# Routing and attention fetches rearranged: most tiles of x read during attention, half of the statistics on ScalarE, groups of 4, 4, 4, 4, 8, 8, one weight load a step, half rows read ahead

## The reference

```
x = x + proj(attention(layernorm(x)))          # 16 heads of 16, rotary, causal mask
z = layernorm(x)
e = argmax(z @ centroids.T)                     # 8 experts, one for each token
y = z + relu(LN_e(z) @ w1[e].T + b1[e]) @ w2[e].T + b2[e]     # 256 -> 1024 -> 256
x = x + alpha * y + (1 - alpha) * z,   alpha = sigmoid(z @ centroids[e])
```

## Time and profile before

| | us |
|---|---|
| median of 3 runs (878.6 to 885.98) | 881.75 |
| the profiled execution | 886.25 |
| its span | 884.5 |
| PE busy | 812.1 |
| DVE busy | 599.5 |
| ACT busy | 508.4 |
| POOL busy | 340.6 |

### The profile page before, as it was taken

The page is one execution under the profiler, slowest core; times in us unless marked ns, Lnnn a source line. Parts: engine busy times, 40 slices in busy tenths (PEclk is TensorE's granted clock), DMA queues, the critical chain, the costliest instruction groups (busy, mean ns, idle before and its releaser), DMA issues. The chain is left out here.

```text
span 884.5 us, 24359 instructions
## 1 busy us (share of the span) xinstructions
PE 812.1 (92%) x8788; PEld 497.3 (56%) x8789; DVE 599.5 (68%) x1161; ACT 508.4 (57%) x1175; POOL 340.6 (39%) x476
## 2 busy tenths in 40 slices
PE   7999859889979999999999988777999999999984
PEld 4555423333334444443344335456999999999853
DVE  5888999779969999999999605754733333333342
ACT  4767427668858888888888892023333333333331
POOL 9999653233333433334343332524111111133211
PEclk9999979999989999999999999988899999999998
DMA  7578532543453343433335115865555555555550
GB/s 281 179 231 255 170 119 69 175 169 53 111 106 91 95 100 97 90 87 86 86 81 159 51 42 180 277 189 196 173 186 182 180 180 183 187 187 189 179 173 4
DMA packets 63355, 128.90 MB, mean 146 GB/s; under 512 B 16982, under 2 KB 44247, under 8 KB 56983
## 3 DMA queue, kind: packets, MB, share of 16 engines
q1 hardware_dynamic: 59094, 112.53, 42.9%
q0 software_dynamic: 4160, 15.03, 4.6%
HBM read 99.89 MB, written 22.98 MB: 139 GB/s over the span
## 5 line engine op out<-in xcount | busy, mean ns | idle before, releaser
L917 ACT ACTIVATE arena<-ps_pair 128x512 f32<-128x512 f32 (+2 forms) x640 | 317.9, 556 | 76.6 <-PE ps_pair L1240 73.7
L997 DVE TENSOR_REDUCE B_block_max<-ps_item 128x8 f32<-128x1024 f32 x288 | 335.4, 1217 | 37.4 <-PE ps_item L1144 37.1
L1240 PE MATMUL ps_pair<-q_stack,k_stack 99*32 99x512 bf16 (+7 forms) x3072 | 198.5, 334 | 9.4 <-DMA q_stack<-B_nm 6.7
L831 POOL TENSOR_SCALAR_AFFINE_SELECT arena<-arena 128x256 f32<-128x256 f32 x256 | 102.4, 409 | 160.2 <-ACT arena L917 158.5
L1257 PE MATMUL ps_pair<-arena,B_v_quad 128*32 128x512 f32 (+3 forms) x1536 | 157.0, 493 | 0.9 <-ACT B_oacc L936 0.7
L1240 PEld LDWEIGHTS ps_pair<-q_stack,k_stack 99*32 99x32 bf16 (+1 forms) x3072 | 69.1, 96 | 130.0 <-ACT arena L917 62.1
L2037 PEld LDWEIGHTS C_bank<-arena 128*128 128x128 f32 x1024 | 122.5, 196 | 5.2 <-ACT arena L1558 3.7
L2037 PE MATMUL C_bank<-arena 128*128 128x128 f32 x1024 | 123.0, 280 | 2.0 <-ACT arena L1558 2.0
L1144 PE MATMUL ps_item<-k_stack,q_stack 64*128 64x128 bf16 (+2 forms) x1280 | 108.2, 267 | 15.9 <-DVE B_block_max L997 8.9
L2061 PE MATMUL C_ps_p<-arena 128*128 x512 | 117.4, 381 | 3.2 <-issue 3.1
L1588 ACT ACTIVATE arena<-C_bank,ffn_columns 128x128 f32<-128x128 f32 x128 | 36.6, 368 | 116.8 <-PE C_bank L2037 108.0
(11 more groups left out here) (204 smaller groups left out, 777.0 us busy)
## 6 DMA issues: line engine op xcount, KB each, us to landing
arena<-in_w_exp SPq DMA_DIRECT2D x41, 1024.0 KB
qk_parts<-arena SPq DMA_DIRECT2D x32, 384.0 KB, 3.4
q_stack<-qk_parts SPq DMA_DIRECT2D x96, 128.0 KB, 3.3
k_stack<-qk_parts SPq DMA_DIRECT2D x64, 128.0 KB, 3.4
arena<-in_w_exp POOLq DMA_DIRECT2D x6, 1024.0 KB, 7.1
rows<-payload SPq DMA_DIRECT2D x32, 130.5 KB
arena<-in_x SPq DMA_DIRECT2D x8, 512.0 KB, 4.7
arena<-in_x_feat SPq DMA_DIRECT2D x8, 512.0 KB, 5.7
```

What stands on the lines that cost most here:

```text
L831: pool.affine_select(out=block_p, in_=block_p, compare_op=ALU.is_ge, fill=0.0, base=0, pattern=[[0, 2], [1, P]], channel_multiplier=-1).th ...
L917: act.activation(pr[s % PR][:, h:h + 2 * n - 1:2, 0:W], ps_s[(EXPS * Q.const + exps_to[s] + u) % R][:, 0:n * W].rearrange("p (h n) -> p h ...
L997: dve.tensor_reduce(bmx[:, g:QH:GH, first:first + 3 * gap + 1:gap], src[:, :, :].rearrange("p c (b n) -> p c b n", n=P), AX.X, ALU.max).th ...
L1240: mm = pe.matmul(bank[at:at + 32, :], ks[rows, r, half, bass.ds(g * SEQ + kb * P + at, 32)], qs[rows, r, half, bass.ds(g * SEQ + c * QW + ...
```

## The change

- `GROUPS` is (4, 4, 4, 4, 8, 8), not (4, 4, 4, 4, 6, 6, 4); four groups are scattered within the loop over pairs, the other two from slots 0 and 1. The token numbers (`COL_ID`) are copied group by group, before each group's scatters.
- Of the 32 tiles of x, 24 are read in step 14 of attention, in three transfers of 1 MB: two into a ring slot of the q and k stacks that is free by then, one into the last sequence's values (`load_early`). `add` reads them there. The other 8 tiles are read in the routing stage, now behind `place_out`, `store_inverse` and `spread_inverse` of step 15. b2 is read once four pairs are added.
- `stats` of the even pairs 0 to 14 go to ACT: an ACTIVATE Copy for the mean and an ACTIVATE Square for the variance of each tile, with accumulation, and one to scale the means.
- DVE inverts step 15's sums at pair 4 (was 2) and normalizes the last outputs at pair 10 (was 7).
- In attention, `place_out(n-2)` comes behind the maxima of step n in SP's queue. The pad regions are written three each in steps 5, 7 and 9, between `spread_inverse` and `load`. w2 is read in steps 1, 2, 3, 4, 5 and 14, at sub-block 4.
- Rows of half slots have a buffer each and are read in steps 24 to 30, before `load_rows` would read them.
- The first normalization (slot 0) stands ahead of the last pair of ACT's statistics; the table's scratch rows are in another tile.

```diff
-GROUPS = (4, 4, 4, 4, 6, 6, 4)
+GROUPS = (4, 4, 4, 4, 8, 8)
...
+        def load_early(sp):
+
+            sp.wait_ge(s_vq, NQ)
+            for i in range(3):
+                sp.dma_start(x_early[i][:, :, :], x[i * KB * P:(i + 1) * KB * P, :].rearrange("(t p) n -> p t n", p=P)).then_inc(s_early[i], 16)
...
+        def load_half_rows(sp, k):
+            at = sp.value_load(slot_tab[0:1, 1, bass.ds(FULL + k, 1)], min_val=0, max_val=DUMMY_ROW + HT)
+            sp.dma_start(half_rows[:, k, 0:P],
+                         pay_d[bass.ds(at, HT), 0:DIM].rearrange("t (a n) -> a t n", a=DC)).then_inc(s_rh[k], 16)
+            sp.dma_start(half_rows[:, k, P:P + PAYW - DIM],
+                         pay_d[bass.ds(at, HT), DIM:PAYW].unsqueeze(0).to_broadcast([DC, HT, PAYW - DIM])).then_inc(s_rh[k], 16)
...
-        early_at = (1, 1, 2, 2, 14, 14)
+        early_at = (1, 2, 3, 4, 5, 14)
+        W2_AT = 4
...
-                    if n.const >= 2:
-                        place_out(sp, n.const - 2, out_ring(n.const - 2))
                     if n.within(NQ):
 
                         wait(sp, s_n3, n, 1, 1)
                         for half in range(2):
                             sp.dma_start(qs[SROWS[half]:SROWS[half] + MROWS, n.ring(R), half, :],
                                          nm[half * MAXR // 2:(half + 1) * MAXR // 2, :]).then_inc(s_row, 16)
+                    if n.const >= 2:
+                        place_out(sp, n.const - 2, out_ring(n.const - 2))
                     if n.const == 2:
                         load_bias_rows(sp)
-                    if n.const == 4:
-                        sp.wait_ge(s_pad0, 2)
-                        for e in range(NE + 1):
-                            sp.dma_start(pay_d[e * REGION:e * REGION + P, :], padrow).then_inc(s_pad, 16)
                     if n.const >= 3:
                         spread_inverse(sp, n.const - 3)
+                    if n.const in (5, 7, 9):
+                        if n.const == 5:
+                            sp.wait_ge(s_pad0, 2)
+                        for e in range(3 * (n.const - 5) // 2, 3 * (n.const - 5) // 2 + 3):
+                            sp.dma_start(pay_d[e * REGION:e * REGION + P, :], padrow).then_inc(s_pad, 16)
                     Q = n + 2
                     if Q.within(NQ):
                         load(Q)
+                    if Q.const == NQ:
+                        wait(sp, s_s, Q, QH * SUB, -QH * SUB * (R - 1))
+                        load_early(sp)
...
-                        if k == NM_AT + 1:
+                        if k == W2_AT:
...
+        BY_ACT = [u for u in range(NP - 1) if u % 2 == 0]
...
-                    t = h * G // 2
+                place_out(sp, NQ - 1, o_last)
+                store_inverse(sp, NQ - 1)
+                spread_inverse(sp, NQ - 1)
+                for h in range(len(s_x)):
+                    t = X_LATE + h * G // 2
                     sp.dma_start(xr[:, t:t + G // 2, 0:DIM],
                                  x[t * P:(t + G // 2) * P, :].rearrange("(t p) n -> p t n", p=P)).then_inc(s_x[h], 16)
-                    if h == 0:
-                        place_out(sp, NQ - 1, o_last)
-                    if h == 4:
-                        store_inverse(sp, NQ - 1)
-                    if h == 5:
-                        spread_inverse(sp, NQ - 1)
                 sp.dma_start(col[:, :, :], cols).then_inc(s_fl, 16)
+                sp.wait_ge(s_x2, KB // 2)
                 sp.dma_start(b2r[:, :], b2.partition_broadcast(P)).then_inc(s_fl, 16)
...
+                    if n.reg is None and COPY_AT <= n.const < COPY_AT + HALVES:
+                        load_half_rows(sp, n.const - COPY_AT)
...
-                pool.tensor_copy(xr[:, :, COL_ID].bitcast(I32), cst[:, C_ID32:C_ID32 + NT].bitcast(I32)).then_inc(s_id, 1)
-                pool.wait_ge(s_id, 1)
                 for g in range(NG):
                     pool.wait_ge(s_ps, g + 1)
                     pool.wait_ge(s_sb, 4 * (g + 1))
                     pool.wait_ge(s_x2, starts[g + 1] // 2)
+                    pool.tensor_copy(xr[:, of(g), COL_ID].bitcast(I32),
+                                     cst[:, C_ID32 + starts[g]:C_ID32 + starts[g + 1]].bitcast(I32)).then_inc(s_id, 1)
+                    pool.wait_ge(s_id, g + 1)
...
+                def stats(u):
+                    act.wait_ge(s_x2, u + 1)
+                    for t in (2 * u, 2 * u + 1):
+                        i = t % 2
+                        act.activation(junk[:, i, :], xr[:, t, 0:DIM], ACT.Copy, scale=1.0 / (HD * DIM),
+                                       accum_out=am[:, t:t + 1]).then_inc(s_am, 1)
+                    if tiles_by(True, u):
+                        act.wait_ge(s_va, tiles_by(True, u))
+                    for t in (2 * u, 2 * u + 1):
+                        done = tiles_by(True, u) + t % 2 + 1
+                        act.wait_ge(s_am, done)
+                        act.activation(junk[:, 2 + t % 2, :], xr[:, t, 0:DIM], ACT.Square, bias=am[:, t:t + 1], scale=-1.0 / HD,
+                                       accum_out=mv[:, t, 1:2]).then_inc(s_va, 1)
+                    act.activation(mv[:, 2 * u:2 * u + 2, 0], am[:, 2 * u:2 * u + 2], ACT.Copy, scale=float(HD)).then_inc(s_ma, 1)
+
+                for u in range(NP - 1):
+                    if u == NP - 3:
+                        act.wait_ge(s_fl, 32)
                         act.wait_ge(s_tab, 2)
-                    if NP - 1 - RD <= w < NP - 1:
-                        expert_of(act, Step(w - (NP - 1 - RD)), known)
+                        normalize(Step(0))
+                        for S in range(RD):
+                            expert_of(act, Step(S), known)
+                    if u in BY_ACT:
+                        stats(u)
...
-                    if u == 2:
+                    if u == 4:
                         invert_sums(dve, NQ - 1)
-                    if u == 7:
+                    if u == 10:
                         normalize_out(dve, NQ // 2 - 1)
-                    if u % 2 == 0 and 2 <= u <= 2 * FIRST_GROUPS:
-                        positions(u // 2 - 1)
-                        row_scalars(u // 2 - 1)
-                    if u % 2 == 1 and u < 2 * FIRST_GROUPS:
-                        one_hot(u // 2)
-                    if u < 2 * FIRST_GROUPS:
+                    for g in range(NG - 2):
+                        if u == ends_at[g] + 2:
+                            positions(g)
+                            row_scalars(g)
+                            if g == FIRST_GROUPS - 1:
+                                first_table()
+                    for g in range(NG - 1):
+                        if u == ends_at[g] + (0 if g < FIRST_GROUPS else 2):
+                            one_hot(g)
+                    if u < NP - 1 and u not in BY_ACT:
                         stats(u)
-                    if u == 2 * FIRST_GROUPS:
-                        first_table()
-                    if u > 2 * FIRST_GROUPS:
-                        stats(u - 1)
-                    if u == starts[FIRST_GROUPS + 1] // 2:
-                        one_hot(FIRST_GROUPS)
-                    if u in (2 * FIRST_GROUPS + 2, 2 * FIRST_GROUPS + 4):
+                    if u in (NP - 4, NP - 2):
                         dve.wait_ge(s_tab, 2)
-                        expert_of(dve, Step(u // 2 - FIRST_GROUPS - 1), known)
-                    if u == starts[FIRST_GROUPS + 1] // 2 + 2:
-                        positions(FIRST_GROUPS)
-                        row_scalars(FIRST_GROUPS)
-                    if u == starts[FIRST_GROUPS + 2] // 2:
-                        one_hot(FIRST_GROUPS + 1)
+                        expert_of(dve, Step((u - (NP - 4)) // 2), known)
...
```

More of the change, by code:

```diff
@@ L347, in program @@
         rows = ctx.enter_context(nc.sbuf_tensor("rows", [P, RD, PAYW], F32))
+        half_rows = ctx.enter_context(nc.sbuf_tensor("half_rows", [P, HALVES, P + PAYW - DIM], F32))
+        s_rh = [sem(f"half_rows_loaded{k}") for k in range(HALVES)]
         def load_rows(sp, S):
-            at = sp.value_load(slot_tab[0:1, 1, bass.ds(S.value(), 1)], min_val=0,
-                               max_val=DUMMY_ROW + (HT if is_half(S) else 0))
-            if is_half(S):
[L353 to L356, removed]
-            else:
-                sp.dma_start(rows[:, S.ring(RD), :], pay_d[bass.ds(at, P), :]).then_inc(s_rl[S.ring(RD)], 16)
@@ L1296, in phase_route_experts, with tiles_by @@
         FT = sum(FIRST)
-        assert starts[NG] == NT and all(k % 2 == 0 and k <= G for k in GROUPS) and all(k == 4 for k in FIRST)
+        assert starts[NG] == NT and all(k % 2 == 0 and k <= G for k in GROUPS)
+        ends_at = [starts[g + 1] // 2 - 1 for g in range(NG)]
+        BY_ACT = [u for u in range(NP - 1) if u % 2 == 0]
+        def tiles_by(act, u):
+            return 2 * sum((m in BY_ACT) == act for m in range(u))
         assert (FT * P - NE * (P - 1) + P - 1) // P >= FIRST_SLOTS
```

(27 more changed lines are left out.)

79 lines of the change are left out of this document (45 added, 34 removed).

## The result

The changed kernel takes 926.9 us (median; 925.4 to 931.1) against 881.5 (878.6 to 886.0) of the kernel before: a ratio of 1.049 (95% interval 1.045 to 1.053), **slower**. The forecast was 871, faster or the same; of the rivals the fourth had the right sign and place, but its 895 was too small. The profiled execution has a span of 924.3 us, 39.8 more than before, at a clock of 0.949 (before 0.967).

A forecast was written before the change was run, and what follows sets the result against it. PE was taken to bound the kernel, busy 812.1 of 884.5 us. Attention -3.7, routing -7, scatters +5 and half slots -4.9 gave -10.6: 875.6 profiled, 871 on the median's scale; range 857 to 885.

The forecast's parts named there:

- Attention, what goes: Attention: PE's waits for maxima and pads, with the clock lost behind them, go: 10.1 and 8.2, together 18.3 us won.
- Attention, what comes: Attention: place_out behind the maxima and moved pads and biases delay the stacks: 3.2, 8.4 and 3, together 14.6 us lost.
- Rival 4: Attention: SP makes PE wait in all twelve steps until the clock falls, 38 us lost: 899, median's scale 895; chance 0.08.
- Rival 1: Attention: SP's issues don't bind, so none of the 14.6 us comes: 861.0, on the median's scale 857; chance 0.20.
- Routing: Routing stage: x there sooner and POOL's scatters nearly without gaps, the last ending at 568.6: 7 us won, bounds 2 and 12.
- a sign of being wrong: Routing: the forecast is wrong if slot 0 starts no sooner behind the end of attention than 57 us.
- Rival 3: Routing: not shortened, the fourth group's landing decides and w2 and w1 crowd it; 2 us won, not 7: 876; chance 0.16.
- rival 2: Slots and routing: POOL's runs hold PE fully, 7.6 or 8 us lost, routing wins only 2: 879; chance 0.20.
- Scatters during slots: Slots: PE's semaphores arrive late in POOL's run of 16 scatters: 5 us lost, between 0 and 7.6.
- The sentence that the later stores cost nothing: Slots: stores behind the scatters come later too, but a result's buffer is written again only two slots later.
- Half slots: Half slots at the end: rows come before slot 31, steps take 4.65 us: 4.9 us won, bounds 3 and 5.

The follow-up runs named there:

- a_order_back: The changed kernel with place_out of step n ahead of the wait for the maxima again: 0.991 of the kernel before.
- b_spread: The kernel before with the maxima first, then spread_inverse, then place_out, then the stacks: 1.019 of the kernel before.
- second and third set: Eight of the twelve follow-up kernels, four a set; the kernel before, run beside them, took 873.2 and 875.7 us.
- a_groups: The changed kernel with place_out ahead of the maxima again and the routing groups of the kernel before (6, 6, 4): 0.984 of the kernel before.
- b_dose_alt: The kernel before with 4, 8, 12, 16 small SP transfers ahead of the stack loads in steps 7, 9, 11, 13: steps of 23.9, 26.2, 27.1, 28.1 us; no ratio.
- first set: Four of the twelve follow-up kernels, run on one chip; the kernel before, run beside them, took 888.7 us.

## Why the prediction was wrong

**Attention, what goes: right in what left, not in what it was worth.** The waits for the maxima and for the pads left. But of the 18.3 us the two edits together bring 9.2 in attention (392.8 to 383.6, `a_order_back`), since the w2 reads at their new places meet the stack loads of SP's steps 3 to 5 and cost 7.7 there. That meeting was no term of the sum.

**Attention, what comes: wrong, and this is the step that failed.** It took 0.4 us for an ordinary step with a bound of 8 us for all eight; SP's steps 6 to 13 lost 3.8 us each in the mean, and the six of them without pads 3.7. In step 13, which has no pads and follows a step that left the maxima on time (4.7 us behind item 0), the parts lie open:
- SP's order: stacks at 13.1 behind item 0, forecast 12.9. Right; 2.0 later than the 11.1 of the kernel before.
- Issue: 10.67 us for the 14 transfers, against 9.84 before in the mean: 0.8, not in the sum.
- Landing: 3.74 us behind the end of the last issue, against 1.87 before in the mean: 1.9, not in the sum, since the earlier trace rows were read as a property of the loads. `b_spread` shows that they depend on how long `spread_inverse` has been issued.
- The 1.1 us to spare come off: 2.0 + 0.8 + 1.9 - 1.1 = 3.6, and the wait was 3.8.

Over SP's steps 6 to 13 the weights differ: the stacks start 3.4 us later in the mean (14.5 behind item 0 instead of 11.1), the issues take 0.4 longer and the landing 1.1, and 1.1 was to spare: 3.8. So the start of the stacks is the largest part, and more than its 1.8 by order alone.

What makes it more is the second omission, the loop. In the changed kernel seven waits of 2.3 to 5.4 us were followed by PE at 1.2 GHz as the next step began (granted clock 0.50 from 453.8 to 460.6 us, around item 0 at 455.03; means over such steps 0.87 to 0.94), maxima ready at 6.0 to 7.0 instead of 4.7 to 4.9, and with `place_out` behind them the next stacks at 13.9 to 15.1, or 16.2 with pads. After waits of 1.0 to 1.5, and after one of 2.8, neither happened; in the other kernels waits of 1.9 to 3.2 us went either way. POOL and SP in SP's step 10, which item 0 opened at 398.42:

```profile
404.36 0.43 POOL L848 TENSOR_TENSOR B_nm<-B_n,B_nr 96x128 bf16<-96x128 bf16 x1
```

```profile
413.48 0.55 SPq L398 DMA_DIRECT2D q_stack<-qk_parts  x1
```

I had priced the clock at 1.7 us of PE's time, once; it is paid a second time through SP. The two bind only together, since in the old order SP stands ahead of the maxima with `place_out` and doesn't wait for them for long.

**Rival 4** named this chain, and its threshold of 2.7 us was for SP's time alone. With the landing 1.9 and the issue 0.8 later, a start 1.8 late is enough to begin it, and once it runs the threshold is passed as well: in five of the six ordinary steps from 6 on the stacks start 2.8 to 4.0 us late. Its size was too small, 38 us lost in attention for 18.3 won, 19.7 net; the changed kernel lost 34.3 net. That ordinary steps had only 1.1 us to spare was in the rows; a chance of 0.08 was too low for it.

**Rival 1** is refuted: the order of issues alone gives 1.051, and eight 4 KB transfers, with next to nothing to move, make a step 2.3 us longer. The Trainium skill (DMA: Bandwidth & Descriptors, Issuing engines are not separate DMA queues) says that the time to initiate a DMA is usually small relative to the DMA itself. Here an issue takes about 0.6 us, a stack load lands in 3.0, and 14 issues in a row take about 10.

**Routing: 7 forecast, none came.** Slot 0's matmuls start 57.2 us behind the first projection, as before, which the prediction had named as a sign of being wrong. The first scatter is 1.7 us earlier (12.4 behind the first projection instead of 14.1), but the sixteenth ends at 39.4, against 40.2. PE's semaphores are late here too: DVE adds at 596.39 what PE had done at 593.31, 1.2 us behind a run of eight scatters. In the second and third set the sixteenth scatter ends at 35.0 in the kernels that read x early, near the 33.1 of the sum, and at 36.7 to 38.1 in the others; yet slot 0's normalization follows 10.3 to 11.2 us later instead of 8.6 to 9.2, so that at most 2 us are won there as well. The traces show where: SP issues the rows of slot 0 as soon as before (6.1 to 6.4 us behind the scatter, 6.3 to 7.4 in the kernels that don't read x early), but the normalization follows this issue by 4.0 to 4.8 us in all seven kernels that read x early, and by 2.2 to 2.3 in the others. `a_groups`, then `b_dose_alt`, SP and ACT:

```profile
569.36 1.45 SPq L355 DMA_DIRECT2D rows<-payload  x2
```

```profile
574.14 0.60 ACT L1575 ACTIVATE arena<-rows 128x256 f32<-128x256 f32 x1 [6.79 <-DMA rows<-payload]
```

```profile
592.17 1.45 SPq L358 DMA_DIRECT2D rows<-payload  x2
```

```profile
594.37 0.60 ACT L1543 ACTIVATE arena<-rows 128x256 f32<-128x256 f32 x1 [6.02 <-DMA rows<-payload]
```

In the kernels that read x early, two reads of w2 and one of w1, 1 MB each, are issued in the 7 us ahead of those rows; in the others the two of w2 are 16 to 17 us ahead and the one of w1 8 to 9. That these reads slow the rows wasn't tried. Rival 3 had the size and by this perhaps the crowding, rival 2 the late semaphores of this run.

**Scatters during slots: 5 forecast, 7.6 measured,** the far bound, from slot 0 to slot 31. The sentence that the later stores cost nothing was wrong: where PE's semaphores are in time, they are the cost.

**Half slots: 4.9 forecast, 5.1 measured,** at 4.6 us a step, forecast 4.65; PE of the changed kernel:

```profile
882.67 1.95 PE L2025 MATMUL C_bank<-arena 128*64 128x256 f32 x16
...
887.29 1.95 PE L2025 MATMUL C_bank<-arena 128*64 128x256 f32 x16
```

**The sum** of what the trace shows is 34.3 + 2.4 + 0.4 + 7.6 - 5.1 and 0.2 before attention, 39.8; forecast were -3.7 - 7 + 5 - 4.9. Without the new order the change would have been worth 0.9%.

## What to carry to other kernels

Idle time of a queue right ahead of transfers that PE waits for may not be spare time: here small transfers could fill it, but the loads landed late once it was gone, because of one transfer ahead of it. So look at the landings with and without the gap before using it up. When an issue is moved behind a semaphore, ask whether that semaphore depends on the engine that will stall; if it does, one stall makes the next, and the price is per step, for every step. A margin of 1 us in a loop of 13 steps deserves a test of how the step answers to a delay before its price is set.

## What was not expected of the hardware

- A transfer of 256 KB to 64 partitions, issued right ahead of 128 KB loads, raised their time from issue to landing from 2.9 us to 5.1; with 5.6 us of other issues between, it did nothing to them. Nine transfers of 130.5 KB at the same place left them at 2.3 to 3.8.
- Late semaphores of PE while POOL issues indirect transfers without a pause: PE's transposes that had ended at 646.0 were seen by ACT at 663.4. The traces of before, of after and of the four kernels of the first set show it, none of the eight in the other two sets does, and with the same groups the kernels that show it take 6 to 11 us more (60.4 to 63.8 against 53.0 to 54.4 for slots 0 to 8). It may be most of why the kernel before takes 881 to 889 us in some runs and 873 to 876 in others, but of the latter there is no trace. It is neither the chip alone, since the first two sets ran on chips of the same number, nor the code. What differs stays open.
